# Weight sums, loads and first products of the dense stage of a pre-norm block put in another order (TensorE-bound kernel, float32 in three passes)

## The chip, the cores and the metric

One core of a Trainium2 chip. The metric is the device time of one execution in microseconds (us), the median of several runs.

## The reference

The input x is 2 x 1024 tokens of 1024 numbers, in float32. Two stages follow, each on the layer-normed x and added to it:

```python
x = x + attn(layernorm(x))      # conv of width 3, 1024 -> 3 x 256 (q, k, v); blocks of 128 tokens;
                                # 16 heads of 64, causal softmax attention inside a block; wo; proj_w to 1024
x = x + ffn(layernorm(x))
...
y = einsum('bth,oh->bto', x, W_base) + b_base
z = einsum('bth,erh->bter', x, lora_A[active])             # 4 active experts of rank 8
contribs = einsum('bter,eor->bteo', z, lora_B[active]) * 2.0
logits = (einsum('bth,eh->bte', x, router_W) + router_b)[..., active]
alpha = softmax(log(domain_prior[active] + 1e-12) + logits)
return y + einsum('bteo,bte->bto', contribs, alpha)
```

The list `active` is an input, so the kernel reads it on the chip before it can load the experts' weights.

## The kernel before

Every large product is made of three float32r products: each operand is split into a high part (ScalarE rounds it) and a low part (VectorE subtracts), and high x high, high x low and low x high are summed in PSUM. Each engine runs one stream of instructions in the order of its block in the code (`@block.sync`, `gpsimd`, `scalar`, `vector`, `tensor`), and semaphores join the streams. Nothing is scheduled by a tool: the order in the code is the order on the engine, and a wait holds up all that stands behind it. SyncE's queue also works in order, so a load behind a wait isn't issued before the wait is over.

The program has three stages.

1. Convolution, up to about 255 us.
2. Attention: `attention_pair(D)` for D = 0 to 32, on TensorE (L1887), VectorE (L1359), ScalarE (L922) and GpSimd (L708). Step D makes the scores of heads pair D - 1, their mask and maximum (`masked`), exponentials, `reciprocals`, GpSimd's scaling of `pr` (L715), and for earlier pairs the turning of the probabilities (`turns`, pair D - 2), the head outputs and the output sums (pair D - 3). Four steps make a group of 256 tokens (g = D // 4, q = D % 4). With q = 3, `a_high` and `a_low` split the group's attention output, GpSimd adds the bias to the group's x rows (`bias_sum`, L703) and the projection begins. `attention_step(g, i)` (L578) is SyncE's side, with J = 8g + i at two J a step. At (1, 0) it loads `fw_raw` (W_base, 24 loads) and then, for each active expert, `a_raw`, `r_raw` and two `lbias`.
3. Dense stage, 16 tiles of 128 tokens. The tiles 0 to 3 (CL = 4) are plain: `dense(t, b)` (L1924) multiplies a tile by block b of three blocks of columns, in 8 chunks. The tiles 4 to 15 go in 6 pairs, each pair by seven block products in place of eight (`product`, L1992: A11, S1, S2, A12, S3, A22, S4). These need sums of blocks of the weights, 4 kinds of 4 rows. They are made during attention: `weight_sum(k)` (L1410) on VectorE, `high_sum(k)` (L956) on ScalarE, `low_sum(k)` (L1423) on VectorE, `store_sum(k)` (L533) on SyncE to DRAM. `load_sums(kind)` (L541) brings them back when attention has left its memory, 8 rows of 266 KB for each kind (the tiles `t_v`, `t_p`, `t_b`, `t_f`). `gate_weights` (L1400) copies the experts' weights into `fw_raw`, in step TFIRST - 1 = 5. The sums follow in the steps 6 to 21.

In the dense stage x comes from DRAM twice: as `x1t` (`load_tile`, L519, 512 KB) for the output sum and the moments, and as `x1g` (`load_groups`, L523) to be scaled and turned on VectorE. For a pair of tiles ScalarE takes the moments (`tile_moments`, L1052), GpSimd makes the factors and writes `spread` (`pair_moments`, L756), TensorE's `pair_moments(q)` (L1984) spreads them over the partitions by a small matmul, and ScalarE scales `x1g` (`pair_scale`, L1062). Then `pair_turn`, the block sums and the splits follow on VectorE. The gate of a tile goes through `gate_scores`, `gate_exponential`, `gate_inputs`, a transpose (`gate_turn`), `gate_turned` and `low_rank` (L2018). In `b_stack` lie the split `lora_B` and the bias.

## Time and profile before

| | us |
|---|---|
| median of 3 runs (lowest to highest) | 792.14 (791.73 to 792.81) |
| the profiled execution | 790.63 |
| its span, first to last instruction | 788.9 |
| TensorE busy | 756.0 (96%) |
| VectorE busy | 563.8 (71%) |
| ScalarE busy | 454.4 (58%) |
| GpSimd busy | 176.3 (22%) |

The mean granted TensorE clock was 0.989. The profiled execution lies 1.5 us below the median. In the profile's rows PE is TensorE's matmuls, DVE is VectorE, ACT is ScalarE, POOL is GpSimd and SPq is SyncE issuing DMAs. L12 is line 12 of the kernel. A matmul's duration overlaps the next ones, so the distance from start to start tells what one costs.

### The profile page before, as it was taken

How to read it: one execution, taken by the hardware profiler on the slowest of the kernel's cores; microseconds unless marked ns; L12 is line 12 of the kernel's file. 1: busy time of each engine (PE TensorE's matmuls, PEld its weight loads, DVE VectorE, ACT ScalarE, POOL GpSimd, SP SyncE). 2: the span in 40 equal slices, each digit the busy share in tenths (PEclk: the TensorE clock that was granted, in tenths of full speed). 3: DMA queues.
4: the chain of work that ended last, by engine and by line, in shares of the span. 5: the costliest groups of instructions: out<-in, count | busy, mean ns of one | idle time of the engine just before them, and what ended most of it. 6: DMA issues, size and time to landing. Idle time of an engine off the chain costs nothing. (4 is left out here: it accounts for less than half of the span.)

```text
span 788.9 us, 15051 instructions
## 1 busy us (share of the span) xinstructions
PE 756.0 (96%) x5326; PEld 677.9 (86%) x5326; DVE 563.8 (71%) x1503; ACT 454.4 (58%) x1180; POOL 176.3 (22%) x204
## 2 busy tenths in 40 slices
PE   4999999999999997999999999999999969999997
PEld 3898888888888886898889889999988959999997
DVE  7999995889887845757575755456687446777874
ACT  5953442344334884687777776677871166666540
POOL 3300100000000233435261626262420111222200
PEclk9999999999999998999999999999999989999998
DMA  8745844434446283343424241402147937334402
GB/s 332 281 133 165 270 126 140 163 112 160 161 147 241 88 259 85 101 144 98 162 98 162 88 172 56 160 2 107 60 142 232 357 106 246 124 138 140 154 36 81
DMA packets 61246, 118.86 MB, mean 151 GB/s; under 512 B 11507, under 2 KB 30067, under 8 KB 59892
## 3 DMA queue, kind: packets, MB, share of 16 engines
q1 hardware_dynamic: 59156, 110.56, 41.8%
q0 software_dynamic: 2016, 7.34, 2.3%
q8 instruction: 43, 0.70, 0.4%
q14 instruction: 31, 0.25, 0.1%
HBM read 82.68 MB, written 34.80 MB: 149 GB/s over the span
## 5 line engine op out<-in xcount | busy, mean ns | idle before, releaser
L715 POOL TENSOR_TENSOR pr<-pr,rrec 128x512 f32<-128x512 f32 x64 | 66.6, 1042 | 215.6 <-DVE rrec L1310 212.9
L883 ACT ACTIVATE pr<-pr,negmax 128x128 f32<-128x128 f32 x256 | 99.0, 394 | 8.5 <-DVE negmax L1302 8.5
L1767 PE MATMUL net_psum<-ua,wa 128*128 128x256 f32 x384 | 83.8, 379 | 0.6 <-DVE ua L1192 0.6
L1767 PEld LDWEIGHTS net_psum<-ua,wa 128*128 128x128 f32 x384 | 72.6, 190 | 10.4 <-issue 0.8
L63 PE MATMUL net_psum<-x_hi,w_hi 128*128 128x512 f32 x192 | 76.4, 398 | 0.0
L64 PE MATMUL net_psum<-x_lo,w_hi 128*128 128x512 f32 x192 | 76.2, 397 | 0.0
L65 PE MATMUL net_psum<-x_hi,w_lo 128*128 128x512 f32 x192 | 75.6, 394 | 0.0
L840 ACT ACTIVATE w_hi<-raw 128x1024 fp32r<-128x1024 f32 x24 | 25.5, 1062 | 85.4 <-PE net_psum L65 76.6
L63 PE MATMUL net_psum<-c_hi,wqk_hi 128*128 128x256 f32 x256 | 74.2, 290 | 0.0
L64 PE MATMUL net_psum<-c_lo,wqk_hi 128*128 128x256 f32 x256 | 71.6, 280 | 0.0
L65 PE MATMUL net_psum<-c_hi,wqk_lo 128*128 128x256 f32 x256 | 71.5, 279 | 0.0
L1302 DVE CUSTOM_DVE_ANT_0 pr<-net_psum,mask 128x128 f32<-128x128 f32 x256 | 56.9, 284 | 11.6 <-PE net_psum L1829 11.6
L883 ACT ACTIVATION_READ_ACCUMULATOR pr<-pr,negmax 128x1 f32 x256 | 49.6, 194 | 0.0
L64 PEld LDWEIGHTS net_psum<-c_lo,wqk_hi 128*128 128x128 f32 x256 | 48.2, 188 | 1.3
L63 PEld LDWEIGHTS net_psum<-c_hi,wqk_hi 128*128 128x128 f32 x256 | 48.1, 188 | 1.2
L1310 DVE RECIPROCAL rrec<-rsum 128x4 f32<-128x4 f32 x64 | 11.3, 177 | 52.3 <-ACT pr L883 52.1
L65 PEld LDWEIGHTS net_psum<-c_hi,wqk_lo 128*128 128x128 f32 x256 | 48.2, 188 | 0.0
L902 ACT ACTIVATE oT_hi<-net_psum,net_bv_c 128x256 fp32r<-128x256 f32 x64 | 26.9, 472 | 32.2 <-PE net_psum L1840 31.6
L65 PEld LDWEIGHTS net_psum<-x_hi,w_lo 128*128 128x128 f32 x192 | 36.3, 189 | 8.7
L64 PEld LDWEIGHTS net_psum<-x_lo,w_hi 128*128 128x128 f32 x192 | 36.2, 188 | 8.5
L63 PEld LDWEIGHTS net_psum<-x_hi,w_hi 128*128 128x128 f32 x192 | 35.9, 187 | 8.8
L1576 DVE TENSOR_TENSOR x1t<-net_psum,x1t 128x528 f32<-128x528 f32 (+1 forms) x48 | 32.1, 689 | 15.7 <-PE net_psum L2003 15.7
(268 smaller groups left out, 2283.3 us busy)
## 6 DMA issues: line engine op xcount, KB each, us to landing
wa<-in_conv_w SPq DMA_DIRECT2D x24, 512.0 KB, 3.9
raw<-in_conv_w SPq DMA_DIRECT2D x24, 384.0 KB, 4.2
xn<-in_x SPq DMA_DIRECT2D x16, 512.0 KB, 10.1
xr<-in_x SPq DMA_DIRECT2D x8, 1024.0 KB, 5.1
x_scratch<-xr SPq DMA_DIRECT2D x8, 1024.0 KB, 4.3
x1t<-x_scratch SPq DMA_DIRECT2D x16, 512.0 KB, 4.7
x1g<-x_scratch SPq DMA_DIRECT2D x56, 128.0 KB, 2.9
c_raw<-c_scratch SPq DMA_DIRECT2D x7, 768.0 KB, 5.2
```

Of the source, the lines that this page charges most:

```text
L63: pe.matmul(out, w_hi, x_hi, start=first, stop=False)
L64: pe.matmul(out, w_hi, x_lo, start=False, stop=False)
L65: return pe.matmul(out, w_lo, x_hi, start=False, stop=last)
L715: pool.tensor_tensor(pr[:, jj % 4], pr[:, jj % 4], rrec[:, jj % 4].unsqueeze(2).to_broadcast([P, UN, P]), ALU.mult).then_inc(s["p_ready"], 1)
L840: act.activation(w_hi[:, k % WR], raw[:, k % RR, 1:5], ACT.Copy).then_inc(s["w_hi_ready"], 1)
L883: e = act.activation(pr[:, jj % 4, un], pr[:, jj % 4, un], ACT.Exp, bias=negmax[:, jj % 2, un:un + 1], scale=-1.0, accum_out=rsum[:, jj % ...
L902: act.activation(oT_hi[:, jj % 2], op[:, jj % 2].rearrange("p b t -> p (b t)"), ACT.Identity, bias=bv_c[:, jj % NP:jj % NP + 1]).then_inc( ...
L1302: m = dve.tensor_tensor_reduce(out=pr[:, jj % 4, un], in0=scp[:, h, jj % 2 * GT + b * P:jj % 2 * GT + (b + 1) * P], in1=mask[:], scale=-DH ...
L1310: dve.reciprocal(rrec[:, jj % 4], rsum[:, jj % 2]).then_inc(s["rrec_ready"], 1)
L1576: dve.tensor_tensor(half_of(tile, j), bank_half(b, j), half_of(tile, j), ALU.add).then_inc(s["y_ready"], 1)
L1767: mm = pe.matmul(duo_acc(d, mi)[:, v * QUADS:(v + 1) * QUADS], wa[:, a % AW, mi, 1 - v, c % 2], ua[:, c, v, n * QUADS:(n + 1) * QUADS], st ...
```

## The change

No instruction is added or left out but in what pieces the products are cut. It moves work in seven places:

- SyncE at (1, 0): the experts' weights are loaded ahead of the 24 loads of `fw_raw`, no longer behind them.
- `TFIRST` is 8 in place of 6, so `gate_weights` stands at the end of step 7. The 16 sums are placed by `sum_at(k)`: four for every group, two in the step with q = 0, one each with q = 1 and q = 2, none with q = 3. Three of the four stand ahead of `unit_out(D, 0)` and the reciprocals, the second (k % 4 = 1) at the end of the step. Their stores follow in SyncE's order, and the loads of tiles 0 and 1 stand behind the last store.
- The loads at the beginning of the dense stage: a tile of x, its groups and one kind of weight sums take turns.
- The moments of tiles 4 and 5 are taken one tile earlier on ScalarE, and GpSimd makes `spread` ahead of a store. TensorE's `pair_moments(0)` stands ahead of `dense(3, 0)`, and `pair_moments(1)` behind half of A12.
- `dense(0, 0)` and `dense(0, 1)` are interleaved by chunks from chunk 3.
- In pairs that have a next one, ScalarE's `gate_exponential(a + 1)` comes ahead of `gate_turned(a)`.
- In the last pair the gates are turned and the low-rank products made between the chunks of S4.

```diff
-    TFIRST, TSUMS = 6, 16
+    TFIRST, TSUMS = 8, 16
+    SPREAD = 3
+    def sum_at(k):
+        return TFIRST + DG * (k // 4) + (0, 0, 1, 2)[k % 4]
+
+    def sums_in(D, late):
+        return [k for k in range(TSUMS) if sum_at(k) == D and (k % 4 == 1) == late]
...
+            def load_into_free(t):
+
+                old = max((i for i in range(t) if x_slot(i) == x_slot(t)), default=None)
+                if old is None:
+                    for par in range(2):
+                        sync.wait_ge(y_stored[par], 16 * (CL // 2))
+                elif old < CL:
+                    sync.wait_ge(s["y_ready"], NB * (old + 1))
+                else:
+                    p = (old - CL) // 2
+                    sync.wait_ge(pair_stored[p % 2], 32 * (p // 2 + 1))
+                load_tile(t)
...
-                k = (NP * g + i) // 2 - TFIRST - 1
-                if i % 2 and 0 <= k < TSUMS:
-                    store_sum(k)
-                if (g, i) == (5, 7):
+                for k in range(TSUMS):
+                    if NP * g + i == 2 * sum_at(k + 1) + 2:
+                        store_sum(k)
+                if NP * g + i == 2 * sum_at(TSUMS) + 2:
...
                     sync.dma_start(act_sb[:], active).then_inc(s["active_loaded"], 16)
-                    for c in range(DC):
-                        for (lo, hi), off, (left, right) in zip(COLS, OFF, OUT):
-                            sync.dma_start(fw_raw[:, row(c), ...], ...)
                     sync.wait_ge(s["active_loaded"], 16)
                     for e in range(E_ACT):
...
+                    for c in range(DC):
+                        for (lo, hi), off, (left, right) in zip(COLS, OFF, OUT):
+                            sync.dma_start(fw_raw[:, row(c), ...], ...)
...
-            load_sums(0)
-            for t in range(XS, CL):
...
-            if CL == XS:
-                load_sums(1)
-            load_sums(2)
-            load_pair(0)
-            load_pair(1)
+            for t in range(XS, CL + 3):
+                load_into_free(t)
                 load_groups(t)
+                if t < XS + 3:
+                    load_sums(t - XS)
+            load_groups(CL + 3)
+            load_into_free(CL + 3)
             load_sums(3)
...
@@ gpsimd, tiles
-                store(t)
                 if t == CL - 2:
                     pair_moments(0)
+                store(t)
@@ scalar, attention_pair
-                if 0 <= D - TFIRST < TSUMS:
-                    high_sum(D - TFIRST)
+                for k in sums_in(D, False) + sums_in(D, True):
+                    high_sum(k)
@@ scalar, tiles
+                if t == CL - 1:
+                    pair_gs(0)
+                    pair_scale(0, 0)
                 if t:
                     gate_exponential(t)
+                if t == CL - 2:
+                    tile_moments(CL + 1)
                 if t == CL - 1:
-                    pair_scale(0)
+                    pair_scale(0, 1)
                 gate_turned(t)
...
-                if t == CL - 2:
+                if t == CL - 3:
                     tile_moments(CL)
-                    tile_moments(CL + 1)
@@ scalar, pairs
-                gate_turned(a)
-                gate_exponential(a + 1)
+                if more:
+                    gate_exponential(a + 1)
+                    gate_turned(a)
+                else:
+                    gate_turned(a)
+                    gate_exponential(a + 1)
@@ vector, attention_pair
                 for jj in pair_of(D - PV):
                     heads_low(jj)
+                weight_sums(D, False)
...
-                if 0 <= D - TFIRST < TSUMS:
-                    weight_sum(D - TFIRST)
-                if 0 <= D - TFIRST - 1 < TSUMS:
-                    low_sum(D - TFIRST - 1)
+                weight_sums(D, True)
...
+            def weight_sums(D, late):
+                for k in sums_in(D, late):
+                    weight_sum(k)
+                    if k:
+                        low_sum(k - 1)
+                if D == sum_at(TSUMS) and not late:
+                    low_sum(TSUMS - 1)
@@ vector, tiles
+                    else:
+                        pair_turn(0, 0)
                     gate_scores(t)
...
                 if t == CL - 1:
-                    pair_turn(0, 0)
                     pair_turn(0, 1)
@@ tensor
-            dense(0, 0)
+            dense(0, 0, range(SPREAD))
+            for c in range(SPREAD, DC):
+                dense(0, 0, (c,))
+                dense(0, 1, (c - SPREAD,))
             for jj in pair_of(ND - 1):
                 output_sums(jj)
-            dense(0, 1)
+            dense(0, 1, range(DC - SPREAD, DC))
...
+                    else:
+                        pair_moments(0)
                     dense(t, 0)
-                    if t == CL - 1:
-                        pair_moments(0)
                     dense(t, 1)
...
-                if q + 1 < NQ:
+                if 0 < q and q + 1 < NQ:
                     pair_moments(q + 1)
...
                 product(q, A12, YB, range(0, 2))
+                if q == 0:
+                    pair_moments(1)
...
+                else:
+                    gate_turn(a)
+                    product(q, S4, ZB, range(0, 1))
+                    low_rank(q, 0, (0,))
+                    product(q, S4, ZB, range(1, 3))
+                    gate_turn(a + 1)
+                    product(q, S4, ZB, range(3, 4))
+                    low_rank(q, 0, (1,))
+                    low_rank(q, 1)
```

The order on the queues, as a listing of the compiled instructions gives it (line, operation, target<-source, shape). First SyncE at the place of `attention_step(1, 0)`, before (the three shapes of `fw_raw` come eight times, the last five rows four times):

```order
L472 DMA c_raw<-c_scratch 128x6x256
L602 DMA act_sb<-in_active 1x4
L605 DMA fw_raw<-in_w_base 128x248
L605 DMA fw_raw<-in_w_base 128x512
L605 DMA fw_raw<-in_w_base 128x264
...
L608 TENSOR_LOAD act_sb
...
L609 DMA a_raw<-in_lora_a 128x8x8
...
L610 DMA r_raw<-in_router_w 128x8
...
L611 DMA lbias<-in_router_b 128x1
L612 DMA lbias<-in_prior 128x1
```

and of the change:

```order
L479 DMA c_raw<-c_scratch 128x6x256
L606 DMA act_sb<-in_active 1x4
L609 TENSOR_LOAD act_sb
...
L610 DMA a_raw<-in_lora_a 128x8x8
...
L612 DMA lbias<-in_router_b 128x1
L613 DMA lbias<-in_prior 128x1
...
L616 DMA fw_raw<-in_w_base 128x264
L589 DMA pb_r<-in_pb 128x1024
L591 DMA xr<-in_x 128x2x1024
```

The small loads now come straight behind the list of experts, and the bias row and x rows (`pb_r`, `xr`) stand behind the weights, no longer behind the small loads.

SyncE at the end of attention, of the change (before, `xr`'s store is followed by all 24 rows `t_...`, then four groups' loads each of two tiles, then both `x1t`):

```order
L586 DMA x_scratch<-xr 128x2x1024
L528 DMA x1t_145<-x_scratch 128x1024
L538 DMA x1g_170<-x_scratch 32x4x256 x4
L567 DMA t_v_183<-t_scratch 128x532
...
L567 DMA t_v_190<-t_scratch 128x532
L528 DMA x1t_146<-x_scratch 128x1024
L538 DMA x1g_171<-x_scratch 32x4x256 x4
L567 DMA t_v_191<-t_scratch 128x532
```

Tile 4's x (`x1t_145`) stands ahead of the first eight rows of sums, tile 5's (`x1t_146`) behind them.

VectorE in step 10 and at the beginning of step 11 (q = 3), of the change:

```order
L1328 SCALAR_TENSOR_TENSOR oT_lo<-net_psum,net_bv_c,oT_hi 128x256 x2
L1433 TENSOR_TENSOR t_raw<-fw_raw,t_raw 128x532
L1445 TENSOR_TENSOR t_low<-t_raw,t_hi 128x532
L1355 COPY vf<-net_psum 128x512
L1324 RECIPROCAL rrec<-rsum 128x4 x2
L1355 COPY vf<-net_psum 128x512
L1316 ISA pr,negmax<-net_psum,mask 128x128
```

Before, `t_raw` and `t_low` stand behind the second copy to `vf`, right ahead of the masks of step 11, and once more at the end of step 11.

## Rows read from the trace of the kernel before

**Rows 1.** who TensorE waited for: reader <- releaser: us in total, times, longest.

```profile
PE net_psum L1990 <- POOL spread L768: 7.3, 2, 6.6
PE net_psum L1882 <- DVE oT_lo L1314: 5.5, 1, 5.5
PE net_psum L63 <- DVE a_lo L1321: 1.1, 3, 0.4
PE net_psum L63 <- DVE fw_lo L1587: 1.1, 2, 0.6
```

**Rows 2.** TensorE's timeline, steps 6 and 7: start, us, line, operation, [idle before].

```profile
307.62 0.58 PE L1882 MATMUL net_psum<-oT_hi,wo_hi 128*128 128x256 f32 x1 [5.49 <-DVE oT_lo L1314]
...
314.14 1.09 PE L1852 MATMUL net_psum<-ident,pr 128*128 128x128 f32 x8
```

**Rows 3.** the same view, steps 10 to 12.

```profile
351.55 0.28 PE L1882 MATMUL net_psum<-oT_hi,wo_hi 128*128 128x256 f32 x1
...
353.05 1.16 PE L1829 MATMUL net_psum<-kf,qf 64*128 64x128 f32 x16
...
355.17 1.09 PE L1852 MATMUL net_psum<-ident,pr 128*128 128x128 f32 x8
...
363.75 1.16 PE L1829 MATMUL net_psum<-kf,qf 64*128 64x128 f32 x16
```

**Rows 4.** VectorE's timeline, end of step 5.

```profile
303.87 0.09 DVE L1403 MEMSET fw_raw<- 128x32 f32 x1 [10.85 <-DMA lbias<-in_prior]
```

**Rows 5.** SyncE's timeline (DMA issues).

```profile
276.00 12.26 SPq L605 DMA_DIRECT2D fw_raw<-in_w_base  x24
...
289.29 0.68 SPq L609 DMA_DIRECT2D a_raw<-in_lora_a  x1
...
301.04 0.38 SPq L612 DMA_DIRECT2D lbias<-in_prior  x1
...
301.94 0.42 SPq L587 DMA_DIRECT2D xr<-in_x  x1
```

**Rows 6.** the tile `xr` from 296 to 320 us, its load.

```profile
DMA to landing us min/median/max: 6.8/6.8/6.8
```

**Rows 7.** GpSimd: timeline of step 11, and the page's group of its scaling.

```profile
355.02 5.22 POOL L706 TENSOR_TENSOR xr<-xr,pb_r 128x1024 f32<-128x1024 f32 x2
...
L715 POOL TENSOR_TENSOR pr<-pr,rrec 128x512 f32<-128x512 f32 x64 | 66.6, 1042 | 215.6 <-DVE rrec L1310 212.9
```

**Rows 8.** VectorE's timeline, end of step 10.

```profile
353.30 2.33 DVE L1425 TENSOR_TENSOR t_low<-t_raw,t_hi 128x532 fp32r<-128x532 f32 x1
```

**Rows 9.** last projection: timelines of TensorE, VectorE and SyncE.

```profile
593.13 0.39 PE L63 MATMUL net_psum<-pw_hi,a_hi 128*128 128x512 f32 x1
...
588.98 1.49 DVE L1321 SCALAR_TENSOR_TENSOR a_lo<-net_psum,net_bcb_c,a_hi 128x128 fp32r<-128x128 f32 x4 [0.59 <-ACT a_hi L919]
...
594.23 0.58 SPq L629 DMA_DIRECT2D b_stack<-b_lo  x1
```

**Rows 10.** tiles 2 and 3: chain, a window (third last column: clock), timelines.

```profile
621.59 9.84 DMA x1t<-x_scratch
...
638.00:642.00 4.00, 4.00 (x12) 3.23 (x13) 1.07 (x1) 3.42 (x8) 0.00 (x0) 0.56 0.00 0
...
624.82 0.28 ACT L1097 ACTIVATE azsT<-net_psum 98x128 fp32r<-98x128 f32 x1 [3.78 <-PE net_psum L2043]
...
615.39 1.35 DVE L1583 TENSOR_TENSOR y<-net_psum,x1t 128x248 f32<-128x248 f32 x3 [2.74 <-PE net_psum L2050]
...
627.54 0.63 PE L2050 MATMUL net_psum<-b_stack,azsT 98*128 98x248 f32 x3
```

**Rows 11.** a later pair: timelines of ScalarE and TensorE.

```profile
714.43 0.30 ACT L986 ACTIVATE expl<-logit,fnegmax 128x4 f32<-128x4 f32 x1
...
715.51 0.64 PE L2027 MATMUL net_psum<-b_stack,azsT 98*128 98x248 f32 x4
```

**Rows 12.** TensorE's timeline, the end.

```profile
783.17 0.74 PE L2027 MATMUL net_psum<-b_stack,azsT 98*128 98x248 f32 x4 [0.37 <-ACT azsT L1097]
```

More of the change, by code:

```diff
@@ L560, in load_sums @@
                         sync.dma_start(to.bitcast(F32), t_dram[kind, part, c]).then_inc(s["t_loaded"], 16)
-            def load_pair(q):
-                for t in (CL + 2 * q, CL + 2 * q + 1):
-                    load_groups(t)
-                for t in (CL + 2 * q, CL + 2 * q + 1):
-                    old = max((i for i in range(t) if x_slot(i) == x_slot(t)), default=None)
-                    if old is None:
-                        for par in range(2):
-                            sync.wait_ge(y_stored[par], 16 * (CL // 2))
-                    elif old < CL:
-                        sync.wait_ge(s["y_ready"], NB * (old + 1))
-                    else:
-                        p = (old - CL) // 2
-                        sync.wait_ge(pair_stored[p % 2], 32 * (p // 2 + 1))
-                    load_tile(t)
+            def load_into_free(t):
[9 more added lines that the diff above has]
+                load_tile(t)
             def attention_step(g, i):
@@ L602, in attention_step @@
                     sync.dma_start(act_sb[:], active).then_inc(s["active_loaded"], 16)
-                    for c in range(DC):
-                        for (lo, hi), off, (left, right) in zip(COLS, OFF, OUT):
-                            sync.dma_start(fw_raw[:, row(c), lo + off:lo + off + right - left], w_base[:, c, left:right]).then_inc(s["fw_loaded"], 16)
                     sync.wait_ge(s["active_loaded"], 16)
@@ L612, in attention_step @@
                         sync.dma_start(lbias[:, 1, e:e + 1], prior[bass.ds(expert, 1), :].to_broadcast([P, 1])).then_inc(s["az_loaded"], 16)
+                    for c in range(DC):
+                        for (lo, hi), off, (left, right) in zip(COLS, OFF, OUT):
+                            sync.dma_start(fw_raw[:, row(c), lo + off:lo + off + right - left], w_base[:, c, left:right]).then_inc(s["fw_loaded"], 16)
                 if (g, i) == (8, 0):
@@ L1127, in _ @@
                 if more:
-                    pair_scale(q + 1)
+                    pair_gs(q + 1)
+                    pair_scale(q + 1, 0)
+                    pair_scale(q + 1, 1)
                     high_operand(q + 1, A11)
@@ L1922, in tile_transposes, with dense @@
                     tr.then_inc(s["fturned"], 1)
-            def dense(t, b):
+            def dense(t, b, chunks=range(DC)):
                 lo, hi = COLS[b]
-                if b == 0:
+                if b == 0 and chunks[0] == 0:
                     pe.wait_ge(s["xT_lo_ready"], 2 * (t + 1))
                     wait(pe, s["y_ready"], NB * (t - 1))
-                if t == 0 and b == 0:
+                if t == 0 and b == 0 and chunks[0] == 0:
                     pe.wait_ge(s["max_ready"], NJ)
@@ L1935, in dense @@
                     pe.wait_ge(s["pT_ready"], NJ)
-                for c in range(DC):
+                for c in chunks:
                     if t == 0 and b == 0:
@@ L1940, in dense @@
                                     fw_hi[:, row(c), lo:hi], fw_lo[:, row(c), lo:hi], c == 0, b == 0 and c == DC - 1)
-                if b == 0:
+                if b == 0 and chunks[-1] == DC - 1:
                     mm.then_inc(s["z_done"], 1)
@@ L2016, in gate_turn, with low_rank @@
                 pe.transpose(bank[0:KB, 0:P], azs[:, t % 2].bitcast(F32), ident[:]).then_inc(s["azT_done"], 1)
-            def low_rank(q, k):
+            def low_rank(q, k, halves=(0, 1)):
                 t = CL + 2 * q + k
                 pe.wait_ge(s["azsT_ready"], t + 1)
-                for j in range(2):
+                for j in halves:
                     new = k == 1 and j == 1
```

36 lines of the change are left out of this document (17 added, 19 removed).

## The prediction

> **What bounds the kernel now.** I read the page first: TensorE is busy for 96% of a span of 788.9 us, so only its pauses and its slow stretches can be won back. Then the list of who waited for whom on TensorE [rows 1]: one wait of 6.6 us for `spread`, one of 5.5 us for `oT_lo`, three of 0.4 us for `a_lo`, two together 1.1 us for `fw_lo`. The start of the program (the longest wait, for `xn`) isn't touched. Last come the timelines around each pause. The profiled execution took 790.63 us against a span of 788.9 us, and the median of the runs shown is 792.14 us. I make the sum as a difference and take it from both. The median carries the forecast. A measurement of this kernel can tell some 0.2% (1.6 us) from no change.
>
> I call the steps of the attention loop (`attention_pair(D)`) steps 0 to 32. Four make a group of tokens.
>
> **Part 1: gate weights.** VectorE's `gate_weights` stands at the end of step 5 and waited 10.85 us, until 303.87 us [rows 4], for small loads. These are queued on SyncE behind 24 loads of `fw_raw`, which took 12.26 us to issue [rows 5]. VectorE works in order, so `oT_lo` came late, and TensorE stood for 5.49 us and then ran slowly [rows 2]. From the first output sum to the turning of probabilities in the next step it took 314.14 - 307.62 = 6.52 us, where the same piece takes 355.17 - 351.55 = 3.62 us four steps later [rows 3]. Together 5.49 + 6.52 - 3.62 = **8.4 us**. In the change the small loads go first and the copy moves to step 7, some 20 us after its old place, so this wait must go. `fw_raw` itself is first read in step 8.
>
> What is late next? The small loads need the list of active experts, whose landing was hidden behind the 24 issues. Now SyncE stands for it. The nearest row is the last small load: issued at 301.04, it released VectorE at 303.87, so 2.8 us. Everything behind on that queue moves by as much, and `xr` stands there [rows 5]: issued at 301.94, now 304.7 us, while TensorE comes earlier by more than 8 us. It took 6.8 us to land [rows 6], so 311.5 us. GpSimd adds the bias to `xr` at the head of its step 7, two adds of together 5.22 us [rows 7], and only then scales the probabilities of that step, at 1042 ns a piece [rows 7]: 317.8 and 318.8 us. TensorE begins step 7 at 307.62 - 5.49 + 1.50 = 303.6 us and step 8 some 10.3 us later (363.75 - 353.05, less the wait of 0.4 inside). It turns the first probabilities 2.1 us into the step [rows 3]: 316.0 us. It would wait 1.8 us, and 0.5 more at the second. VectorE stands before its unit of step 7 at that time, and without it the adds are quicker, down to some four times 1.04 = 4.2 us, which leaves 1.2 us of waiting. Bounds: 0, if `xr` lands 2.5 us sooner, and 3.8 us, if it waits 1.5 us behind the 24 weight loads. I take **1.5 us lost**, between the two values that the rows give.
>
> **Part 2: the weight sums.** Today one sum of `fw_raw` halves and its low part stand at the end of each of the steps 6 to 22. Beside GpSimd's work one such instruction took 2.33 us [rows 8]. That delays the mask of the next step and with it `a_lo`, and TensorE waits three times [rows 1]. After the change no sums stand in the fourth step of a group, nor late in the step before. The three waits go: 1.1 us and some 0.07 us of slower start each, **1.3 us** (bounds 0.4 and 1.4). The early place is a gap in which VectorE waits for TensorE, so the sums cost nothing there. If the gap is gone they push `rrec`, which has a step of slack on TensorE. SyncE's stores of the sums move along and gate the buffer two sums later: rival C.
>
> **Part 3: the first dense blocks.** Block 1's first five chunks now run between chunks 3 to 7 of block 0, so that `fw_lo` of the last chunks is there in time: +1.3 us with the restarts. But the 15 matmuls of 512 columns at 0.23 us put off all that follows block 0 (the gate, the last output sums, then `a_hi`, `a_lo`) by 3.5 - 1.3 = 2.2 us. `a_lo` ended at 588.98 + 1.49 and now at 592.7, while TensorE wants it at 593.13 - 1.3 = 591.8 us [rows 9]: 0.9 us of waiting. `b_stack`, whose last copy was issued at 594.23 [rows 9], is cut from the same VectorE queue, behind `a_lo`. At 596.4 us and with the 2.8 us of a small load it lands at 599.2, and TensorE, after 24 projection matmuls, is there at 592.7 + 5.5 = 598.2. Another 1.0 us. Net **0.5 us lost** (bounds: 1.3 gained, where neither wait shows, and 1.5 lost).
>
> **Part 4: tile 3 and the loads of x.** The pause of 6.6 us [rows 1] is GpSimd's `spread` for tiles 4 and 5. It needs the moments, these need `x1t`, and `x1t`, issued after the last of the 24 weight-sum rows, took 9.84 us to land [rows 10]. Behind the pause the mean granted clock was 0.56 from 638 to 642 us [rows 10], near the lower of its two levels (1.2 and 2.4 GHz): 4 x (1 - 0.56) = 1.8 us of work lost. 6.6 + 1.8 = **8.4 us**. In the change tile 4 is loaded ahead of the first eight rows and tile 5 behind them. I followed the new queue in the clock of before. Tile 5 may be issued when tile 1's three sums are done, 615.39 + 1.35 = 616.7 us [rows 10], and on an emptied queue lands within about 3 us. Its moments (2.4 us) then fill a gap of 3.78 us on ScalarE that ends at 624.82 [rows 10], and `spread` follows near 625. TensorE now asks for it before tile 3's first block, right behind the last low-rank part of tile 2, at 627.54 + 0.5 [rows 10]. So 3 us of room. The last eight of the 24 rows wait for tile 4 to be turned, which follows `spread`'s matmul by some 4 us (four scalings and the transpose): 632 us. They take 4.2 us to issue and land near 641. TensorE wants them behind tile 3 (24 matmuls each of 0.13, 0.23 and 0.12 us, and 0.5) and product A11 (3.1): 628 + 11.6 + 0.5 + 3.1, near 643. So 2 us of room. I take all 8.4 us (bounds 5 and 8.4, if either room is missed by 3 us). The same move, with `pair_moments(1)` after half of A12, removes the second wait for `spread`, **0.7 us** (7.3 - 6.6) [rows 1].
>
> **Part 5: last products.** The low-rank parts of the last pair are spread among the products, so the wait of 0.37 us [rows 12] goes, and the last x rows are summed a little sooner: **0.4 us** (0.1 to 0.8). The loads, the stores and the order within the pairs 1 to 4 are otherwise those of before.
>
> **Sum.** 8.4 - 1.5 + 1.3 - 0.5 + 8.4 + 0.7 + 0.4 = 17.2 us. From 792.14: **774.9 us**. From the profiled execution's 790.63: 773.4 us.
>
> **Rivals.**
> A, nothing stands at step 8. `xr` lands by 309 us. For it: GpSimd has the whole of step 7 before. Against: the 6.8 us of [rows 6]. The time is 1.5 us less, 773.4 us. The Trainium skill has a rule that points there (DMA: Bandwidth & Descriptors, section Anatomy of one DMA, SWDGE path): a transfer costs about 2.0 us plus its bytes at 436 GB/s, 4.4 us for `xr`'s 1 MB. It is fitted to GpSimd's path, and the row of this SyncE load, 6.8 us, does not agree. By the rule the sum would be 18.7 us.
> B, the chain at tile 3 is later than I make it. A DMA queue that moved 400 GB/s for 20 us held up `x1t` by 9.84 us, and the same rows still have to pass. Then a wait of 2 to 4 us appears at `spread` or before product S1. With 3 us: 777.9 us.
> C, the stores of the sums. In the steps 9, 13, 17 and 21 VectorE needs a buffer whose store was issued only at the end of the step before. If the store takes over 3 us longer than the gap, the wait reaches TensorE, about 1 us each time, and eats the 1.3 us of part 2 too: 774.9 + 4 + 1.3 = 780.2 us.
> D, the reorder doesn't take the big waits away, because something else held them (VectorE's own backlog at step 6, or the moments at tile 3). One of the two terms of 8.4 us is missing: 783.3 us.
> E, the other side: slower. In five pairs ScalarE now does the second gate exponential before it copies out the first turned gate. If VectorE's maximum comes late, ScalarE stands, and the low-rank matmuls of TensorE wait for `azsT`. Today the exponential starts at 714.43 and TensorE wants `azsT` at 715.51 [rows 11], so with 0.3 us for the copy there is some 0.4 us of room. To cost more than the 17.2 us gained and 1.6 us beyond, it must be late by 18.8 / 5 + 0.4 = 4.2 us in each pair: 794 us and more. VectorE has the maximum ready 0.03 us before, as the exponential starts at once, so this is remote.
>
> **Chances and range.** The forecast 0.45, A 0.2, B 0.18, C 0.08, D 0.07, E 0.02. The range goes from 771.5 us (A, with part 3 at its better bound and more at the end) to 779.0 us (B in full and part of C). It leaves out D, E and most of C. Faster by over 0.2%: all but E and half a percent, 0.97. Within 0.2%: 0.01. Slower: 0.02.
>
> **What would show it.** In the profile after, no wait for `oT_lo` near 302 us and none of 6 us for `spread`; the clock at full in both places; a wait of 1 to 2 us for the scaled probabilities (`pr`) at the turn near 316 us; no waits for `a_lo` in the attention steps but one of 0.9 us near 576 us in its own time; a short one for `b_stack` some 6 us later. I am wrong if a new wait of more than 3 us stands anywhere on TensorE, or if either big wait stays.

## The result, and the profile after

The changed kernel takes 780.4 us (median of 4 runs, 780.2 to 783.3) against 792.2 us for the kernel before in the same job: a ratio of 0.9859, 95% interval 0.9835 to 0.9883. It is faster by 1.4%, 11.8 us. I had forecast 774.9 us and a range of 771.5 to 779.0 us, so 5.5 us of the expected gain are missing, and the result lies outside the range. The profiled execution took 780.25 us with a span of 778.5 us (before 790.63 and 788.9).

The head of the page of the changed kernel (engine, busy time, share of the span, instructions), with the TensorE row and the clock row in 40 slices:

```profile
PE 753.1 (97%) x5326; PEld 675.6 (87%) x5326; DVE 552.2 (71%) x1503; ACT 452.7 (58%) x1180; POOL 173.1 (22%) x204
...
PE   3999999999999999799999999999999999999997
...
PEclk9999999999999999899999999999999999999999
```

One slice is 19.5 us long. Slice 17 is the only one between the start and the end in which TensorE falls below nine tenths. The changed kernel has one hole in this row, and it is not where the old ones were. The list of who waited for whom on TensorE names it (reader <- releaser: us in total, times, longest):

```profile
PE net_psum L1873 <- POOL pr L717: 3.4, 2, 3.0
PE net_psum L2025 <- issue: 1.8, 1, 1.8
PE net_psum L63 <- DVE a_lo L1335: 0.8, 1, 0.8
PE net_psum L63 <- POOL c_lo L698: 0.7, 1, 0.7
```

Set this beside [rows 1]. Both `spread` waits (7.3 us), the one for `oT_lo` (5.5), those for `a_lo` in the attention steps (1.1) and those for `fw_lo` (1.1) are gone. New are 3.4 us for the scaled probabilities `pr` and 0.7 for `c_lo`, all between 315 and 322 us; 1.8 us before product S1, near 641 us; and 0.8 us for `a_lo` at 589 us. I had forecast a wait for `pr`, but 1.5 us in all (bounds 0 and 3.8), and the one for `a_lo` (0.9). My own sign of being wrong, a new wait of more than 3 us, came true: 3.03 us.

The first wait is gone in full. In [rows 2] the piece from the first output sum to the turning of probabilities took 6.52 us behind a wait of 5.49. The same two rows of the changed kernel, with no wait:

```profile
301.98 0.28 PE L1903 MATMUL net_psum<-oT_hi,wo_hi 128*128 128x256 f32 x1
...
305.60 1.09 PE L1873 MATMUL net_psum<-ident,pr 128*128 128x128 f32 x8
```

That is 3.62 us, so 5.49 + 6.52 - 3.62 = 8.4 us were won here.

**The hole at step 8.** TensorE's timeline (start, us, line, operation, idle before in brackets):

```profile
313.63 1.16 PE L1850 MATMUL net_psum<-kf,qf 64*128 64x128 f32 x16
...
318.84 0.66 PE L1873 MATMUL net_psum<-ident,pr 128*128 128x128 f32 x4 [3.03 <-POOL pr L717]
319.90 1.12 PE L1873 MATMUL net_psum<-ident,pr 128*128 128x128 f32 x4 [0.40 <-POOL pr L717]
321.67 0.58 PE L63 MATMUL net_psum<-c_hi,wqk_hi 128*128 128x256 f32 x1 [0.65 <-POOL c_lo L698]
322.05 0.41 PE L64 MATMUL net_psum<-c_lo,wqk_hi 128*128 128x256 f32 x1
...
331.10 1.16 PE L1850 MATMUL net_psum<-kf,qf 64*128 64x128 f32 x16
```

From the scores (`kf,qf`) of one step to those of the next are 331.10 - 313.63 = 17.47 us. Where nothing stands (run e1_x_first, below) the same stretch takes 10.12 us. So **7.35 us are lost here**. The waits make 3.03 + 0.40 + 0.65 = 4.1 of it. The rest is slow matmuls: those of 256 columns last 0.41 us instead of 0.28. The same timeline cut into windows (window, length, busy time and count of TensorE, of its weight loads, VectorE, ScalarE, GpSimd, then the granted clock, DMA share, GB/s):

```profile
318.00:320.00 2.00, 0.76 (x5) 0.52 (x6) 2.00 (x4) 0.47 (x1) 2.00 (x3) 0.97 0.00 0
320.00:322.00 2.00, 1.35 (x5) 0.94 (x6) 2.00 (x18) 0.73 (x2) 1.62 (x1) 0.50 0.00 0
322.00:324.00 2.00, 2.00 (x11) 2.00 (x11) 0.96 (x2) 0.00 (x0) 0.00 (x0) 0.50 0.38 99
324.00:326.00 2.00, 2.00 (x7) 1.71 (x7) 0.00 (x0) 1.36 (x5) 0.00 (x0) 0.50 0.84 295
326.00:328.00 2.00, 2.00 (x13) 1.77 (x13) 0.77 (x2) 2.00 (x12) 0.11 (x1) 0.83 0.02 8
```

The clock fell to half (1.2 of 2.4 GHz) at 319.9 us, 1 us after the wait of 3 us had ended, and stayed there to 326.7 us. In these windows 2 x (0.03 + 0.5 + 0.5 + 0.5 + 0.17) = 3.4 us of work are lost, 0.3 of it in time that was idle anyway.

Why was `pr` late? SyncE's and GpSimd's timelines, the first to be read beside [rows 5], the second beside [rows 7]:

```profile
275.62 0.44 SPq L606 DMA_DIRECT2D act_sb<-in_active  x1
280.73 0.68 SPq L610 DMA_DIRECT2D a_raw<-in_lora_a  x1
...
292.96 11.35 SPq L616 DMA_DIRECT2D fw_raw<-in_w_base  x24
304.36 0.43 SPq L589 DMA_DIRECT2D pb_r<-in_pb  x1
304.83 0.43 SPq L591 DMA_DIRECT2D xr<-in_x  x1
...
313.12 4.67 POOL L708 TENSOR_TENSOR xr<-xr,pb_r 128x1024 f32<-128x1024 f32 x2 [7.10 <-DMA xr<-in_x]
317.74 2.10 POOL L717 TENSOR_TENSOR pr<-pr,rrec 128x512 f32<-128x512 f32 x2
319.81 1.81 POOL L698 TENSOR_TENSOR c_lo<-c_raw,c_hi 128x768 fp32r<-128x768 f32 x1
```

`xr` was issued at 304.83 us, as forecast (304.7), but took 8.2 us to land where it took 6.8 before [rows 6]. It went out while the weights were still moving: from 300 to 310 us the DMA share is 0.99 to 1.08 in every window of 2 us. Before, it was 0.34 or less from 296 to 302 us. Behind it GpSimd's queue reads in order: two adds, two scalings, then half of `c_lo`, and TensorE wants each of the last two.

**The pause at tile 3.** The last weight-sum row (`t_f`) is issued at 634.39, and TensorE stands before S1 until 642.14 us:

```profile
628.66 1.88 SPq L538 DMA_DIRECT2D x1g<-x_scratch  x4
630.58 1.18 SPq L567 DMA_DIRECT2D t_p<-t_scratch  x2
631.81 2.53 SPq L567 DMA_DIRECT2D t_b<-t_scratch  x5
634.39 0.83 SPq L567 DMA_DIRECT2D t_f<-t_scratch  x1
...
642.14 0.36 PE L2025 MATMUL net_psum<-t_v,xT_hi 128*128 128x266 f32 x1 [1.85 <-issue]
```

"issue" means that the profile found no instruction to blame. Two waits stand ahead of this matmul, for VectorE's sums of tile 3 (L2085) and for all 24 rows (L2086). The profile doesn't name VectorE, so I read the pause as a wait for DMA. Run e3_rows_early tests that.

### The profile page after: what moved, and what is told of

Same layout as the page of the kernel before. It is cut to its first block, busy times and chain, and to the rows that moved or that the text cites. A ratio compares the mean times of both kernels' runs of the same rounds, so it can differ in the third digit from the quotient of the medians.

```text
span 778.5 us, 15056 instructions
## 1 busy us (share of the span) xinstructions
PE 753.1 (97%) x5326; PEld 675.6 (87%) x5326; DVE 552.2 (71%) x1503; ACT 452.7 (58%) x1180; POOL 173.1 (22%) x204
## 4 chain that ended last, share of the span: by engine, by line
PE 85%; DVE 4%; SPq 3%; ACT 2%; DMA 2%; issue 2%; POOL 1%; DVEq 0%; ACTq 0%; POOLq 0%
PE net_psum L63 14%; PE net_psum L64 14%; PE net_psum L65 14%; PE net_psum L1788 11%; PE net_psum L2025 5%; PE net_psum L2027 5%; PE net_psum L2026 5%; PE net_psum L1850 4%; PE net_psum L1861 3%; PE net_psum L1873 3%; PE net_psum L1903 2%; PE net_psum L1904 2%; PE net_psum L1905 2%; SPq L616 1%; PE net_psum L1772 1%
```

## The experiments

Theory 1: the missing 5.5 us are two places, step 8 (7.4 us lost, 1.5 forecast) and S1 (2 us lost, none forecast). The rivals are stated with the runs. All runs here are medians of 5 (of e12_gates_as_before, of 4), and each job timed the kernel before again (792.7, 792.0 and 792.6 us).

**e1_x_first.** In SyncE's step (1, 0):

```
 sync.dma_start(act_sb[:], active)...
+sync.dma_start(pb_r[:], pb.to_broadcast([P, DM]))...
+sync.dma_start(xr[:], x_rows(..., 0))...
 sync.wait_ge(s["active_loaded"], 16)
```

> The changed kernel with one edit: pb_r and the first xr are loaded right behind the list of active experts, ahead of the small loads and of the 24 weight loads. Theory 1 (the missing gain is lost at step 8, because xr lands at 313.1 us and GpSimd's two adds, the scaled probabilities and c_lo queue up behind it): the waits for pr (3.4 us) and c_lo (0.7 us) go, the granted clock stays at 1.00 from 314 to 328 us, and 11.1 - 3.7 = 7.4 us are won: 780.4 - 7.4 = 773.0 us, 772 to 774.5. Rival 2 (GpSimd and VectorE are late at step 8 by their own work, since step 7 now holds the gate copies and xr's adds run beside them): xr lands early, but pr is still 2 to 3 us late, and the time is 776 to 779 us.

Measured: 773.2 us, ratio 0.9762 (0.9745 to 0.9779). TensorE waits neither for `pr` nor for `c_lo`, and from scores to scores are 323.96 - 313.84 = 10.12 us. GpSimd's timeline there:

```profile
306.18 4.78 POOL L709 TENSOR_TENSOR xr<-xr,pb_r 128x1024 f32<-128x1024 f32 x2
311.01 1.04 POOL L718 TENSOR_TENSOR pr<-pr,rrec 128x512 f32<-128x512 f32 x1
312.56 1.04 POOL L718 TENSOR_TENSOR pr<-pr,rrec 128x512 f32<-128x512 f32 x1 [0.50 <-DVE rrec L1325]
313.56 1.81 POOL L699 TENSOR_TENSOR c_lo<-c_raw,c_hi 128x768 fp32r<-128x768 f32 x1
```

The adds start 7 us sooner and don't wait for a DMA. Two loads moved in one queue are worth 7.2 us, and rival 2 falls.

**e2_list_early.** In `attention_step`:

```
+                if (g, i) == (0, 0):
+                    sync.dma_start(act_sb[:], active)...
 ...
                 if (g, i) == (1, 0):
-                    sync.dma_start(act_sb[:], active)...
```

> The changed kernel with one edit: the list of active experts is loaded one group of steps earlier (step 0), so that SyncE does not stand for it at the small loads. It takes 5.1 us of standing out of the queue ahead of xr and leaves the rest of it. Theory 1: xr is issued at 299.7 instead of 304.8 us and lands near 307 to 308, before GpSimd's step 7, so the whole 7.4 us come back: 773.0 us (772 to 775). Rival 2: 776 to 779 us. Rival 3 (it is the 24 weight loads in flight that make xr slow, 8.2 us for a landing that took 6.8 before; the issue alone is not it): xr lands at 310 us or later and half of the stall stays, 775 to 777 us.

Measured: 775.4 us, ratio 0.9783 (0.9770 to 0.9797), rival 3's number. The waiting for the list is gone: it is loaded at 271.26 us, and `a_raw` goes out at 276.60 us without standing. But `xr`, issued at 301.23, lands after 8.5 us, and a rest of the stall stays. SyncE, GpSimd and TensorE:

```profile
276.60 0.69 SPq L611 DMA_DIRECT2D a_raw<-in_lora_a  x1
...
301.23 0.43 SPq L593 DMA_DIRECT2D xr<-in_x  x1
...
309.83 4.74 POOL L709 TENSOR_TENSOR xr<-xr,pb_r 128x1024 f32<-128x1024 f32 x2 [3.86 <-DMA xr<-in_x]
...
316.68 0.65 PE L1874 MATMUL net_psum<-ident,pr 128*128 128x128 f32 x4 [0.33 <-POOL pr L718]
318.45 0.39 PE L63 MATMUL net_psum<-c_hi,wqk_hi 128*128 128x256 f32 x1 [1.12 <-POOL c_lo L699]
```

The granted clock is 1.00 in every window from 312 to 326 us, and from scores to scores the stretch loses 325.63 - 313.57 - 10.12 = 1.9 us, its waits and their restarts. That is most of the 2.2 us between the medians of e1_x_first and e2_list_early. So the standing for the list cost some 5 us of the 7.2, and `xr`'s place behind the weights the rest. `xr` went out only 3.6 us sooner (301.23 for 304.83) and landed no faster. That won 5.4 us in the trace, because the waits were now short and the clock didn't fall.

**e3_rows_early.** The last eight rows ahead of tile 6:

```
-                if t < XS + 3:
-                    load_sums(t - XS)
+                if t == XS:
+                    load_sums(0)
+                if t == XS + 1:
+                    load_sums(1)
+                    load_sums(2)
```

> The changed kernel with one edit: the last eight of the 24 rows of weight sums (load_sums(2)) are issued right behind the second eight, ahead of tile 6 and of its wait for tile 4's turned rows. Theory: the 1.85 us that TensorE stands before product S1 at 640 us are the wait for the last of these rows (issued at 635.2 us); it goes, and with the restart 2.0 us are won: 778.4 us (777.9 to 779). Rival: the pause is something else that the profile calls issue (fetching of code, or the operand sum of S1 from VectorE), and stays: 780.4 us.

Measured: 778.1 us, ratio 0.9824 (0.9809 to 0.9839). The last row goes out at 626.78, and no wait before S1 is left in the list of waits. Moving DMAs alone removed a pause that the profile calls "issue": it was the wait for the rows. (The gain of 2.3 us is small against the scatter, and the intervals of this run and of the changed kernel just touch. e4_both against e1_x_first gives 1.9 us for the same edit.)

```profile
626.78 0.45 SPq L567 DMA_DIRECT2D t_f<-t_scratch  x1
```

**e4_both.** Both edits.

> The changed kernel with both edits of e1_x_first and e3_rows_early. If the two losses are independent they add up: 780.4 - 7.4 - 2.0 = 771.0 us (770 to 772.5). If one of them covers the other, or the later stretch is bound by something that comes at a fixed time, less: above 773 us.

Measured: 771.3 us, ratio 0.9735 (0.9722 to 0.9749). The two losses add up, and no pause is left before S1. In e1_x_first and e7_c_lo_first the profile put a pause of 1.5 and 1.6 us there down to VectorE's `x1t`; since the rows' new place alone removes it here, that too was the rows. This kernel is 9.1 us faster than the change as it was made.

**e5_no_weave.** e4_both, and at the junction:

```
-            dense(0, 0, range(SPREAD))
-            for c in range(SPREAD, DC):
-                dense(0, 0, (c,))
-                dense(0, 1, (c - SPREAD,))
+            dense(0, 0)
 ...
-            dense(0, 1, range(DC - SPREAD, DC))
+            dense(0, 1)
```

> The kernel of e4_both (771.3 us) with the first dense blocks in their old order: block 0 whole, the output sums, block 1 whole. Theory: the interleaving trades 1.1 us of waiting for fw_lo against 0.8 us for a_lo, and the traces of before and after have the same 21.8 us from the first dense matmul to the group moments. The two waits for fw_lo come back, the one for a_lo goes, and the time is the same within 0.5 us: 770.8 to 771.8 us. Rival (the interleaving pays in full, 1.3 us, and a_lo's wait is hidden in the modelled ends): 772.3 to 773 us.

Measured: 770.7 us, ratio 0.9733 (0.9720 to 0.9746). The waits are exchanged as expected, and one of 1.0 us for the second `spread`, near 641 us, is new (e11_turned_first has it too, 0.9; e4_both 0.2):

```profile
PE net_psum L63 <- DVE fw_lo L1611: 1.1, 2, 0.6
```

The interleaving costs 0.5 us or nothing; the two intervals overlap. The full gain of 1.3 us doesn't show. This kernel, e4_both, e10_last_as_before and e11_turned_first are the fastest of the study, and these runs don't tell them apart.

**e6_copy_late_only.** The changed kernel with the 24 weight loads in their old place, ahead of the small loads:

```
                     sync.dma_start(act_sb[:], active)...
+                    for c in range(DC): ... fw_raw ...
                     sync.wait_ge(s["active_loaded"], 16)
 ...
-                    for c in range(DC): ... fw_raw ...
```

> The changed kernel with the old order of SyncE's loads (the 24 weight loads ahead of the small loads, whose list then lands behind their issue), and the gate copies at step 7 as changed. Theory: the first wait goes because the copies stand 20 us later, the swap of the loads isn't needed for it; the small loads land near 304 us as before, xr is issued at 302 and lands in 6.8 to 8.6 us, 309 to 310.5 us, as in e2_list_early. So no wait for oT_lo, 0.5 to 1.5 us for pr and c_lo near 317 us at full clock, S1's pause of 1.9 to 2.7 us stays: 774.5 to 776 us. Rival (the swap is what removes the first wait): a wait for oT_lo near 302 us again, 782 us or more.

Measured: 775.4 us, ratio 0.9781 (0.9768 to 0.9794). There is no wait for `oT_lo`. The copy's new place alone removes it, and the swap of the loads, the first thing that the change is about, costs about 5 us. Here `xr` is issued at 302.66 and lands after 7.8 us; TensorE waits 0.75 us for `pr` and 1.12 for `c_lo`, at full clock.

**e7_c_lo_first.** In GpSimd's step 7 the half of `c_lo` goes ahead of the adds:

```
+                if D == 7:
+                    c_low(2, 1)
                 if 0 <= g - 1 < NG - 1 and q == 3:
                     bias_sum(g - 1, 0)
```

> The changed kernel, and in GpSimd's step 7 the second half of c_lo ahead of the two adds to xr: it lies in the 7 us that GpSimd stands for xr anyway. The wait for pr is untouched (it depends on xr alone), the one of 0.65 us for c_lo goes. Theory: c_lo's place in that queue costs 0.65 us plus what the half clock makes of it, up to 1.4 us: 779.0 to 779.8 us. Rival: TensorE gets to it earlier, meets the next late thing at once (another pr, or the slow clock lasts as long), and nothing changes: 780.4 us.

Measured: 777.7 us, ratio 0.9818 (0.9805 to 0.9831), 2.7 us better than the changed kernel and 1.3 more than I gave it at most. TensorE's timeline:

```profile
320.18 0.83 PE L1875 MATMUL net_psum<-ident,pr 128*128 128x128 f32 x4 [4.32 <-POOL pr L719]
321.24 1.11 PE L1875 MATMUL net_psum<-ident,pr 128*128 128x128 f32 x4 [0.23 <-POOL pr L719]
...
323.65 0.41 PE L64 MATMUL net_psum<-c_lo,wqk_hi 128*128 128x256 f32 x1
323.86 0.32 PE L65 MATMUL net_psum<-c_hi,wqk_lo 128*128 128x256 f32 x1
```

In this execution `xr` took 9.7 us to land, so the wait for `pr` is 1.3 us longer, and still the stretch loses 330.01 - 313.68 - 10.12 = 6.2 us, 1.1 less than the changed kernel. At an equal landing that would be 2.4 us, near the 2.7 of the medians. The wait for `c_lo` was 0.65 us of it. The clock gives the rest: it is at half from 320.5 to 323.9 us, 3.4 us, and in the changed kernel from 319.9 to 326.7, 6.8 us. All five executions have a mean granted clock of 0.996 or 0.997, those of the changed kernel 0.991 to 0.995, so this isn't a chance of the profiled one.

**e8_loads_only.** The kernel before with the change's lines of part 4 alone: `load_into_free` and the loop over it, `store` behind `pair_moments(0)`, `pair_gs` and `pair_scale`, `tile_moments`, `pair_turn(0, 0)`, and on TensorE:

```
-                    if t == CL - 1:
-                        pair_moments(0)
+                    else:
+                        pair_moments(0)
                     dense(t, 0)
 ...
                 product(q, A12, YB, range(0, 2))
+                if q == 0:
+                    pair_moments(1)
```

> The kernel before with the fourth part of the change alone: the order of the loads of x and of the weight-sum rows, the moments, the scalings and pair_moments as changed; the gate weights, the weight sums, the first dense blocks and the last products as before. Theory: the wait of 6.6 us for spread and the slow clock behind it go (8.4 us), the second wait for spread goes (0.7 us), and S1 waits 2.0 us: 792.4 - 7.1 = 785.3 us (784.5 to 786). Rival (the parts hang together; by itself it doesn't get ahead because the stretch ends by another limit): above 787 us.

Measured: 784.7 us, ratio 0.9907 (0.9891 to 0.9924), 7.3 us gained. Part 4 works by itself, with a pause of 2.3 us before S1 and the clock at half behind it. The wait for `oT_lo` (6.0 us) stays, as it must. The profiled execution (786.25 us) is 1.5 us longer than the median, and in it TensorE waits four times for `a_lo`, 2.4 us in all, against three times and 1.1 us in [rows 1]. One of 1.23 us at 317.1 us is new. I have no reading of it.

**e9_sum_each_step.** e4_both with:

```
-        return TFIRST + DG * (k // 4) + (0, 0, 1, 2)[k % 4]
+        return TFIRST + k
 ...
-        return [k for k in range(TSUMS) if sum_at(k) == D and (k % 4 == 1) == late]
+        return [k for k in range(TSUMS) if sum_at(k) == D and late]
```

> The kernel of e4_both (771.3 us) with the weight sums as before in their rhythm: one sum and one low part at the end of every step, 8 to 23, on VectorE and ScalarE and in SyncE's stores. Theory: the sums that now fall into the fourth step of a group, or late in the step before it, delay a_lo again, and TensorE waits for it three or four times 0.3 to 0.5 us: 772.3 to 773 us. Rival (xr's early landing has given VectorE enough slack that the rhythm no longer matters): 771.3 us, within 0.4.

Measured: 773.4 us, ratio 0.9762 (0.9749 to 0.9775), 2.1 us slower than e4_both. Of the waits for `a_lo` one (0.8) is the one at the junction that e4_both has too; four stand in the steps, 1.6 us together:

```profile
PE net_psum L63 <- DVE a_lo L1339: 2.4, 5, 0.8
```

**e10_last_as_before** and **e11_turned_first.** e4_both with the `else` branch of the last products taken out and the old end in its place, and e4_both with ScalarE's old order:

```
+            gate_turn(TT - 1)
+            low_rank(NQ - 1, 1)
```

```
-                if more:
-                    gate_exponential(a + 1)
-                    gate_turned(a)
-                else:
-                    gate_turned(a)
-                    gate_exponential(a + 1)
+                gate_turned(a)
+                gate_exponential(a + 1)
```

> The kernel of e4_both (771.3 us) with the last products in their old order: the low-rank parts of both tiles behind all of S4. Theory: 0.3 to 0.4 us slower, 771.6 to 771.7 us, which five rounds can hardly tell from no change. Rival (the last stores go out so much sooner that the end gains over 1 us): 772.3 us or more.

> The kernel of e4_both (771.3 us) in which ScalarE copies out the first turned gate before the second gate exponential in all pairs, as before. Theory: the order is worth nothing, since TensorE has 0.4 us of room in either: 771.3 us within 0.5. Rival E of the prediction, read backwards (the new order costs each of five pairs something): 770.5 us or less. The other rival (the new order serves the next pair's operands and is worth something): above 772 us.

Measured: 771.3 and 771.2 us, ratios 0.9734 (0.9720 to 0.9747) and 0.9732 (0.9719 to 0.9745). Neither edit changes the time by anything that these runs can tell. The end shows why for the first. VectorE's last sums in e4_both, then in e10_last_as_before:

```profile
763.80 1.91 DVE L1600 TENSOR_TENSOR x1t<-net_psum,x1t 128x528 f32<-128x528 f32 x3 [1.09 <-PE net_psum L2055]
```

```profile
762.96 2.60 DVE L1600 TENSOR_TENSOR x1t<-net_psum,x1t 128x496 f32<-128x496 f32 x4
```

The last sum ends at 765.7 us in the one and 765.6 in the other. The new order spreads the sums but doesn't bring the last one forward, since it still follows the last low-rank matmuls.

**e12_gates_as_before.** The changed kernel with the edit of e6_copy_late_only, and:

```
-                if D == TFIRST - 1:
+                if D == 5:
                     gate_weights()
```

> The changed kernel (780.4 us) with the first part undone: the 24 weight loads ahead of the small loads, and the gate copies at the end of step 5. The weight sums keep their new places. Theory: the first part gained 8.4 us at step 6 and lost 7.4 us at step 8, so it was worth 1.0 us: TensorE waits 5 to 6 us for oT_lo near 302 us and not at all for pr near 316 us, and the time is 781.4 us (780.5 to 782.5). Rival (the stall at step 8 belongs to the new places of the sums or to tile 4's part, not to the first part): both stalls show and the time is 786 us or more.

Measured: 781.7 us, ratio 0.9865 (0.9846 to 0.9883). In the list of waits stands the old one, and none for `pr`:

```profile
PE net_psum L1903 <- DVE oT_lo L1328: 5.4, 1, 5.4
```

So the stall at step 8 belongs to the first part and not to the new places of the sums or to tile 4's part. What the first part is worth as a whole is less clear. The medians differ by 1.2 us, but the intervals of this run and of the changed kernel (0.9835 to 0.9883) overlap almost fully. In the traces TensorE restarts before S1 at 642.50 us here and at 642.14 in the changed kernel, so up to there the first part won 0.4 us. Here step 6 costs 5.36 us of waiting and 1.7 of slow clock, 7.1 us, and step 8 gives back 7.35. Behind S1 this execution loses some 1.7 us more, because its pause there, only 0.1 us longer, has the half clock behind it. The restart, and the windows from there:

```profile
642.50 0.56 PE L2025 MATMUL net_psum<-t_v,xT_hi 128*128 128x266 f32 x1 [1.96 <-issue]
...
642.00:644.00 2.00, 1.50 (x7) 1.53 (x8) 0.69 (x1) 0.00 (x0) 0.95 (x3) 0.61 1.01 228
644.00:646.00 2.00, 2.00 (x11) 2.00 (x11) 0.00 (x0) 0.00 (x0) 0.00 (x0) 0.54 1.02 400
```

By these numbers the first part as made is worth some 0 to 1 us, where I had given it 6.9.

## Why the prediction was wrong

Four of the six rows held within 1 us; one was mis-sized by six, one by two.

| term, us gained | forecast | measured | by |
|---|---|---|---|
| part 1, first wait | 8.4 | 8.4 | traces of before and of the change |
| part 1, what is late next | -1.5 | -7.4 | traces; e1_x_first gives -7.2 |
| part 2, sums | 1.3 | 2.1 | e9_sum_each_step against e4_both |
| part 3, dense blocks | -0.5 | -0.5, or 0 | e5_no_weave against e4_both |
| part 4, both `spread` waits | 8.4 + 0.7 | 7.3 | e8_loads_only |
| part 5, end | 0.4 | 0.0 | e10_last_as_before against e4_both |
| sum | 17.2 | 9.9 | change: 11.8 |

The parts leave 1.9 us of the whole unassigned. Most are differences of two medians, taken in different surroundings (part 2, 3 and 5 in e4_both's kernel, part 4 in the kernel before). In e8_loads_only's profile the pause before S1 has 1.6 us of slow clock behind it, and in the changed kernel's it has none. That would be most of the 1.9, but it is read from one execution of each, so it stays open.

**The step that failed is "What is late next?" in part 1.** Its mechanism was right, from the queue on SyncE to `pr`. Its size was put at 1.5 us and measured 7.4, by three omissions.

First, the landing. I took 6.8 us from an execution in which `xr` was issued 14 us behind the 24 weight loads. In the change it goes out right behind them and takes 8.2 us (8.5, 8.6 and 9.7 in e2_list_early, e3_rows_early and e7_c_lo_first, which have that order). I had this at "waits 1.5 us behind the 24 weight loads", as a bound of 3.8 us, and the waits for `pr` were 3.4. So the price was in the text, and I took a lower one. The list of experts took 5.1 us where I wrote 2.8, but the 24 issues took 0.9 less than before (11.35 against 12.26) and the gap of 1.0 behind them fell away, so that 304.7 us came out right by luck.

Second, I stopped at `pr`. GpSimd's next instruction in that queue, `c_lo`, has its own reader on TensorE: 0.65 us more, 1.1 in e2_list_early and e6_copy_late_only.

Third, the clock. I gave the old waits of 5.5 and 6.6 us a slow stretch behind them and the new one none. At 1.8 us of waiting that is right, as e2_list_early and e6_copy_late_only show. At 3 us it cost 3.3 us more. So the upper bound of the term wasn't 3.8 us: with the clock on top it is some 7 us, and the sum with that bound is 780.4 us.

**Part 4: the room of 2 us before S1.** I counted the wait for tile 4's turned rows and then 4.2 us of issues for the eight rows. Between the two stand the four issues of `x1g` for tile 6, 1.9 us, which I left out. The issues themselves took 4.6 us, and from the last one (ended 635.2) to TensorE's restart are 6.9 us, where I had 4.8. Together that is 4.4 us late against 2.2 of room, and TensorE itself came 0.4 us later than I had it: 1.85 us of pause. Rival B named this place and a size (2 to 4 us) that is nearly right. The room before `spread`, 3 us in my sum, was 1.1: `spread` was ready at 623.6 us and TensorE read it at 624.7, since tile 5's `x1t` took 6.2 us to land where I had about 3. (No row stood behind that figure: the fastest of these loads in the kernel before took 3.7.) The room was still enough.

**The rest.** No wait for `oT_lo`, none for `spread`, none for `a_lo` in the steps: right. `a_lo` at the junction: 0.8 us at 589 us, forecast 0.9. Its place, 576 us, was a slip: I took off the whole 17.2 us, of which only 8.2 come before it. With that and the 5.9 us more that step 8 cost it would have been 590. `b_stack`: no wait at all, so that half of part 3's loss wasn't there (its terms, by the way, make 0.6 and not 0.5). The stretch from the first dense matmul to the group moments takes 21.8 us before and after.

Rival A is refuted: `xr` landed at 313.1 us and not by 309. By the fit that the Trainium skill gives for GpSimd's path (DMA: Bandwidth & Descriptors, Anatomy of one DMA) 1 MB would take an estimated 4.4 us. This load of SyncE took 8.2, and 8.9 in e1_x_first, where no weight load is ahead of it. Rival C didn't show: no wait of TensorE stands in steps 9, 13, 17 or 21. That its 780.2 us is next to the measured time is chance. Rival E didn't either, and e11_turned_first shows the order to be neutral.

Part 2 was undersized. I priced the sums by the three waits of the kernel before, but with the new first step and no stall ahead the old rhythm has four, of 0.4 us on average, and costs 2.1 us (e9_sum_each_step), 1.6 of it in the waits.

## What to carry to other kernels

Moving a load ahead of others moves those others back; look at what every load of the queue gates, not only the two that change places. Here the swap was not needed at all, a later place for the copy did it, and the load that had to go first was a third one, `xr`. When a stall is forecast, follow the late engine's queue past the first reader, and ask whether the clock may fall with it: where it did, a stall of 2.0 to 6.6 us cost 1.6 to 3.1 us on top of itself here. A pause that the profile calls "issue" in front of a wait for many DMAs is one for DMAs.

## What the runs showed of the hardware

The price of a pause isn't proportional to its length. Before S1 TensorE stood 1.5, 1.6 and 1.85 us (e1_x_first, e7_c_lo_first, the changed kernel), and the granted clock behind it was 1.00. It stood 1.96, 2.3, 2.7 and 3.5 us (e12_gates_as_before, e8_loads_only, e2_list_early, e6_copy_late_only), and the clock fell to half. Between 1.85 and 1.96 us of pause lie some 1.7 us of lost work. The windows of e2_list_early there; TensorE starts again at 637.55, at full clock, and falls to half 1.5 us later:

```profile
636.00:638.00 2.00, 0.45 (x4) 0.48 (x5) 0.93 (x2) 0.00 (x0) 1.23 (x3) 1.00 1.10 232
638.00:640.00 2.00, 2.00 (x15) 2.00 (x14) 0.00 (x0) 0.00 (x0) 0.00 (x0) 0.76 1.00 354
640.00:642.00 2.00, 2.00 (x11) 2.00 (x10) 0.00 (x0) 0.44 (x1) 0.00 (x0) 0.50 1.05 399
```

At step 8 two or three short pauses, 1.5 us together in e2_list_early and 1.9 in e6_copy_late_only, left it at 1.00. The pauses of more than 1.9 us, read in windows of 0.25 us (work lost: half of the time at half clock in which TensorE had work):

| place | pause, us | clock at half, us | work lost, us |
|---|---|---|---|
| before, step 6 | 5.49, to 307.62 | 306.99 to 313.81 | 3.1 |
| before, tile 3 | 6.57, to 637.90 | 634.66 to 641.49 | 1.8 |
| change, step 8 | 3.03, to 318.84; then 0.40, 0.65 | 319.86 to 326.69 | 3.1 |
| e3_rows_early, step 8 | 3.67, to 319.49; then 0.66 | 318.44 to 325.27 | 2.6 |
| e7_c_lo_first, step 8 | 4.32, to 320.18; then 0.23 | 320.52 to 323.94 | 1.6 |
| e12_gates_as_before, step 6 | 5.36, to 307.69 | 304.51 to 311.34 | 1.8 |
| e8_loads_only, step 6 | 6.01, to 308.08 | 304.75 to 311.58 | 1.8 |
| S1: e12_gates_as_before, e8_loads_only, e2_list_early, e6_copy_late_only | 1.96 to 3.52 | 3.4 us each | 1.6 to 1.7 |

The clock can fall during the pause (e12_gates_as_before, 3.2 us before the restart) or behind it (1.5 us later in e2_list_early), and what falls into the pause costs nothing. So the longer wait often had the lower price. At step 8 it rises with the short pauses behind the first (1.05, 0.66 and 0.23 us), but whether these kept the clock low is not settled by three profiles.

This also goes with the scatter of the times. The three kernels with a pause before S1 of 2.3 us and more in their profiles range over 2.2 to 5.0 us in five executions, and e12_gates_as_before over 3.4 in four. Of the five kernels without one behind a free step 8, three range over 0.4 to 0.6 us and two (e5_no_weave, e4_both) over 1.4 and 1.7. Only one execution of each was profiled, so the link is likely and not shown.

The same 1 MB load of `xr` took different times by what stood ahead of it in the queue:

| ahead of it | landing, us |
|---|---|
| 24 weight loads, the last issued just before | 8.2, 8.5, 8.6, 9.7 (change, e2_list_early, e3_rows_early, e7_c_lo_first) |
| the weight loads and then 14 us of small loads | 6.5, 6.7, 6.8, 7.8 (e8_loads_only, e12_gates_as_before, before, e6_copy_late_only) |
| `c_raw` (768 KB), the list and `pb_r`, no weight load | 8.7 to 8.9 (e1_x_first, e4_both, e5_no_weave, e9_sum_each_step, e10_last_as_before, e11_turned_first) |
| the later loads of `xr`, steps 8 and on | 4.7 to 6.8 (before, the change, e1_x_first, e2_list_early, e3_rows_early, e6_copy_late_only, e7_c_lo_first) |

With the same order the landings still differ by up to 1.5 us. A landing read from one row holds for that order of the queue; the 6.8 us of [rows 6] was the row of another order.
